# Stacking the high and low rows of a 65-row remainder into one product of a split-precision Gram stage

## The reference

```
sq = jnp.sum(xyz * xyz, axis=1)
d2 = sq[:, :, None] + sq[:, None, :] - 2.0 * jnp.einsum('bdn,bdm->bnm', xyz, xyz)
_, idx = jax.lax.top_k(-d2, k)                    # k = 8
...
shortcut = points
p = _lrelu(points)
g = _group_point(p, idx_t)                        # the 8 neighbours' columns
c = jnp.einsum('oi,bin->bon', w_center[i], p)
gn = jnp.einsum('oi,bikn->bokn', w_neighbor[i], g)
points = (c + gn.sum(axis=2)) / (K + 1.0) + shortcut
```

## Time and profile before

| | |
|---|---|
| median of three runs | 321.87 us (321.72 to 322.04) |
| the profiled execution | 321.73 us, of which span 319.9 us |
| TensorE clock granted | 1.00 throughout |
| TensorE busy | 314.8 us (98%) |
| VectorE, ScalarE, GpSimd busy | 251.7, 172.6, 94.0 us |
| Gram stage | about 4.4 to 105 us, with the start of the layers |
| layer steps | about 110.6 us to the end |

### The profile page before, as it was taken

One profiled execution on the slowest core, in us unless ns is written; L12 is line 12 of the kernel. 1 busy time (PEld: TensorE's weight loads), 2 busy tenths in 40 slices (PEclk: granted clock), 3 DMA queues, 4 the chain that ended last, 5 costly groups with the idle time before them and its releaser, 6 DMA issues.

```text
span 319.9 us, 5033 instructions
## 1 busy us (share of the span) xinstructions
PE 314.8 (98%) x1974; PEld 287.5 (90%) x1974; DVE 251.7 (79%) x333; ACT 172.6 (54%) x255; POOL 94.0 (29%) x85
## 2 busy tenths in 40 slices
PE   8999999999999899999999999999999999999996
PEld 6999999999999688898888988888888988889885
DVE  3995799899899969998777767777776767767674
ACT  4557387388377346546584455444554455544530
POOL 2011111101126304433344333443344333443330
PEclk9999999999999999999999999999999999999999
DMA  7979959988950300000300000000000000000113
GB/s 251 315 284 198 267 166 223 237 283 190 261 92 1 66 2 0 2 0 2 66 1 2 1 3 0 0 0 2 0 2 0 2 0 0 2 0 2 67 67 134
DMA packets 17313, 25.52 MB, mean 80 GB/s; under 512 B 9476, under 2 KB 10756, under 8 KB 17288
## 3 DMA queue, kind: packets, MB, share of 16 engines
q1 hardware_dynamic: 15992, 20.46, 21.3%
q0 software_dynamic: 1296, 4.72, 8.2%
HBM read 20.98 MB, written 2.10 MB: 72 GB/s over the span
## 4 chain that ended last, share of the span: by engine, by line
PE 96%; DVE 2%; DMA 1%; issue 0%; ACT 0%; DVEq 0%
PE wide L444 38%; PE wide L323 29%; PE wide L417 18%; PE wide L433 9%; DMA raw<-in_ctx_dram 1%; PE wide L385 1%; PE wide L392 1%; PE wide L373 1%; DVE gram L713 0%; DVE y_lo L757 0%; DVE r_mixed L690 0%; PE wide L396 0%; DVE half_diag L720 0%; ACT g_high L527 0%; DVE state L765 0%
## 5 line engine op out<-in xcount | busy, mean ns | idle before, releaser
L301 POOL TENSOR_TENSOR r_low<-relu,r_high 128x512 fp32r<-128x512 f32 x64 | 83.7, 1331 | 135.7 <-ACT r_high L593 135.7
L444 PE MATMUL wide<-adj,y_hi 128*128 128x512 f32 (+1 forms) x260 | 101.8, 393 | 1.2 <-DVE y_lo L757 1.2
L444 PE MATMUL wide<-adj,y_lo 128*128 128x512 f32 (+1 forms) x260 | 101.7, 393 | 0.0
L598 ACT CAST y_hi<-wide 128x1024 fp32r<-128x1024 f32 x32 | 32.6, 1018 | 89.2 <-PE wide L417 89.2
L750 DVE TENSOR_TENSOR y_rest<-wide,y_hi 128x1024 f32<-128x1024 f32 x32 | 39.1, 1223 | 30.3 <-ACT y_hi L598 30.2
L765 DVE SCALAR_TENSOR_TENSOR state<-wide,state 128x512 f32<-128x512 f32 (+1 forms) x65 | 44.1, 678 | 20.0 <-PE wide L444 19.9
L444 PEld LDWEIGHTS wide<-adj,y_hi 128*128 128x128 f32 x260 | 49.0, 188 | 10.7 <-issue 2.0
L444 PEld LDWEIGHTS wide<-adj,y_lo 128*128 128x128 f32 x260 | 48.9, 188 | 8.7
L593 ACT ACTIVATE r_high<-relu 128x512 fp32r<-128x512 f32 x64 | 40.6, 634 | 2.0
L590 ACT ACTIVATE relu<-state 128x512 f32<-128x512 f32 x64 | 40.2, 627 | 1.5 <-POOL r_low L301 1.5
L757 DVE SCALAR_TENSOR_TENSOR y_lo<-wide,y_rest 128x1024 fp32r<-128x1024 f32 x32 | 39.1, 1222 | 0.0
(11 more groups left out here) (57 smaller groups left out, 285.7 us busy)
## 6 DMA issues: line engine op xcount, KB each, us to landing
raw<-in_ctx_dram SPq DMA_DIRECT2D x23, 512.0 KB, 5.5
g_low<-in_ctx_dram POOLq DMA_DIRECT2D x9, 512.0 KB, 7.9
state<-in_x_dram SPq DMA_DIRECT2D x4, 512.0 KB, 8.9
out_dram<-state SPq DMA_DIRECT2D x3, 512.0 KB, 2.8
w_raw<-in_fside_BxSxS_dram SPq DMA_DIRECT2D x1, 1024.0 KB, 7.8
rest_raw<-in_ctx_dram SPq DMA_DIRECT2D x4, 130.0 KB
raw<-in_ctx_dram SPq DMA_DIRECT2D x2, 256.0 KB, 3.2
turned<-nbr SPq DMA_TRANSPOSE x16, 3.1
```

What stands on the lines that cost most here:

```text
L301: nc.gpsimd.tensor_tensor(r_low[:, n % 3, h, :], relu[:, h, :], r_high[:, n % 3, h, :].bitcast(fp32), ALU.subtract).then_inc(r_low_ready, 1)
L444: mm = nc.tensor.matmul(bank[to][:, cols], part[:, s % 2, q, h * P:(h + 1) * P], adj[:, b, q, cols], start=(q == 0 and part is y_hi), stop ...
L598: nc.scalar.copy(y_hi[:, s % 2, :, :], wide[main_at(s)][:, :].rearrange("p (q o) -> p q o", q=NB))\
```

## The change

For the first 64 of the 65 rows of the rest, high and low parts are put one above the other in a new tile `rest_both` (rows 0 to 63 high, 64 to 127 low). One product of 128 rows then gives hh + ll of those rows. The 65th row is left over. Its low and high part are put twice below the 65 mixed rows in a new tile `rest_left`, as rows 65 to 68, and their counterparts in `rest_mixed` are multiplied by -SHIFT and by -1, so that the mixed product of 69 rows adds -(SHIFT + 1)(hh + ll) of that row, which UNMIX turns into hh + ll.

The rows go to other partitions by DMA. GpSimd issues five DMAs per item (`rest_copies`): 64 rows of the high part, 64 rows of the low part, twice 2 rows of 512 (4 KB), and the 65 rows of the mixed part (130 KB). ScalarE multiplies rows 64 to 68 by a column of factors (`last_rows`). TensorE's `main_products(b, 6)` waits for the first two DMAs and has one group of four matmuls where there were two, and `mixed_products(b, 6)` waits for ScalarE. `rest_high` and `rest_low` become halves of one tile. VectorE sets the factors at the start (three memsets). The load of the next item's rest also waits for the last-row copies. Two pairs of calls change places at the start of the layers: `copy_adj(2)` goes ahead of `copy_low(3)` on ScalarE, and `y_low(0)` ahead of `relu_mixed(1)` on VectorE.

```
+        rest_parts = sb("rest_parts", [P, 2, N], fp32r)
+        rest_low, rest_high = rest_parts[:, 0, :], rest_parts[:, 1, :]
+        rest_both = sb("rest_both", [P, N], fp32r)
+        rest_left = sb("rest_left", [P, N], fp32r)
+        factors = sb("factors", [P, 1], fp32)
...
         # SP, load_unit, b > 0, k == 6
                         sp.wait_ge(main_summed, b * NB)
+                        sp.wait_ge(last_rows_landed, 32 * b)
...
+            def rest_copies(b):
+                if b > 0:
+                    pool.wait_ge(main_summed, b * NB)
+                pool.wait_ge(g_high_ready[PAIRS], b + 1)
+                pool.dma_start(rest_both[0:HALF, :], rest_high[0:HALF, :]).then_inc(rest_both_landed, 16)
+                pool.wait_ge(g_low_ready[PAIRS], b + 1)
+                pool.dma_start(rest_both[HALF:P, :], rest_low[0:HALF, :]).then_inc(rest_both_landed, 16)
+                if b > 0:
+                    pool.wait_ge(mixed_summed, b * NB)
+                for first in (REST, REST + 2):
+                    pool.dma_start(rest_left[first:first + 2, :], rest_parts[HALF:REST, :, :]).then_inc(last_rows_landed, 16)
+                pool.wait_ge(g_mixed_ready[PAIRS], b + 1)
+                pool.dma_start(rest_left[0:REST, :], rest_mixed[0:REST, :]).then_inc(rest_left_landed, 16)
...
+            rest_copies(0)
             for b in range(1, B):
                 for k in BY_DMA:
                     points_low(b, k)
+                rest_copies(b)
             for n in range(B * LAYERS):
                 relu_low(n)
...
             def main_products(b, k):
+                if k == PAIRS:
+                    pe.wait_ge(rest_both_landed, 32 * (b + 1))
+                    for i in ROWS:
+                        product(i, [rest_both], 0, MAIN_BANK, start=False, stop=True).then_inc(main_summed, 1)
+                    return
...
             def mixed_products(b, k):
+                if k == PAIRS:
+                    pe.wait_ge(rest_scaled, b + 1)
+                    for i in ROWS:
+                        nc.tensor.matmul(sums_of(i, MIXED_BANK), rest_left[0:LEFT, i * P:(i + 1) * P],
+                                         row_of(i, rest_mixed[0:LEFT, :]), start=False, stop=(i != ROWS[0]))\
+                            .then_inc(mixed_summed, 1)
+                    return
...
+            def last_rows(b):
+                act.wait_ge(factors_set, 3)
+                act.wait_ge(last_rows_landed, 32 * (b + 1))
+                act.wait_ge(rest_left_landed, 16 * (b + 1))
+                nc.scalar.mul(rest_mixed[HALF:LEFT, :], rest_left[HALF:LEFT, :], factors[HALF:LEFT, 0:1])\
+                    .then_inc(rest_scaled, 1)
...
             points_parts(1, 3)
+            last_rows(0)
             weights_high(2)
...
                     points_parts(b + 1, 2)
+                    last_rows(b)
                     points_parts(b + 1, 3)
...
                     relu_parts(1)
+                    last_rows(b)
                     copy_main(b)
...
                 if s == 1:
+                    copy_adj(B - 2)
                     copy_low(B - 1)
-                    copy_adj(B - 2)
...
             diagonals(B - 1)
+            y_low(0)
             relu_mixed(1)
-            y_low(0)
```

More of the change, by code:

```diff
@@ L53, in knn_blocks_kernel @@
     SHARE = (1.0 + 1.0 / SHIFT) / (K + 1)
-    assert PAIRS == 6 and 0 < REST <= P and NB == 4 and CH == 2 and K == 8
+    assert PAIRS == 6 and 0 < REST == P // 2 + 1 and NB == 4 and CH == 2 and K == 8
     UNITS = PAIRS + 1
+    HALF = P // 2
+    LEFT = REST + 4
     BY_DMA = (1, 3, 5)
@@ L93, in knn_blocks_kernel @@
             pass
-        rest_low = sb("rest_low", [P, N], fp32r)
-        rest_high = sb("rest_high", [P, N], fp32r)
+        rest_parts = sb("rest_parts", [P, 2, N], fp32r)
+        rest_low, rest_high = rest_parts[:, 0, :], rest_parts[:, 1, :]
+        rest_both = sb("rest_both", [P, N], fp32r)
+        rest_left = sb("rest_left", [P, N], fp32r)
         rest_mixed = sb("rest_mixed", [P, N], fp32r)
+        factors = sb("factors", [P, 1], fp32)
         gram = sb("gram", [P, NB, N], fp32)
@@ L180, in knn_blocks_kernel @@
         first_in = sem("first_in")
+        rest_both_landed = sem("rest_both_landed")
+        rest_left_landed = sem("rest_left_landed")
+        last_rows_landed = sem("last_rows_landed")
+        factors_set = sem("factors_set")
+        rest_scaled = sem("rest_scaled")
         unit_in = [sem(f"unit_in_{k}") for k in range(UNITS)]
@@ L345, in main_products @@
                     for i in ROWS:
[L346 to L350, removed]
-            def mixed_products(b, k):
+                        mm = product(i, low, t, MAIN_BANK, start=False)
+                mm.then_inc(main_used, 1)
+            def mixed_products(b, k):
+                if k == PAIRS:
[5 more added lines that the diff above has]
+                    return
                 mixed = tiles_of(k, g_mixed, rest_mixed)
@@ L359, in mixed_products @@
                             pe.wait_ge(gram_ready, (b - 1) * NB + FREED[n])
[L360 to L364, removed]
+                        mm = product(i, mixed, t, MIXED_BANK, start=(k == 0 and t == 0))
+                mm.then_inc(unit_used, 1)
             def turn_weights(l):
@@ L766, in update @@
                                                op0=ALU.mult, op1=ALU.add).then_inc(state_ready, 1)
+            nc.vector.memset(factors[HALF:P, :], -1.0).then_inc(factors_set, 1)
+            dve.wait_ge(factors_set, 1)
+            nc.vector.memset(factors[HALF:REST + 2, :], -SHIFT).then_inc(factors_set, 1)
+            dve.wait_ge(factors_set, 2)
+            nc.vector.memset(factors[HALF:REST, :], 1.0).then_inc(factors_set, 1)
             for k in range(UNITS):
```

## The result

The changed kernel takes 326.93 us (median of four runs, 325.86 to 328.56), the kernel before 321.87: a ratio of 1.0145, with a 95% interval of 1.0116 to 1.0174. It is slower by about 5 us. The forecast was 320.2 us, with a range up to 324.0, and is wrong in its sign as well as in its size. The profiled execution took 327.0 us, of which the span is 325.2.

A forecast was written before the change was run, and what follows sets the result against it. TensorE was taken as the bound, busy 314.8 of 319.9 us. Three items gaining 0.59 each (1.77) less 0.1 lost at the join gave -1.7 us, so 320.2 us for the median, range 319.0 to 324.0.

The forecast's parts named there:

- The size is that of the first, so I take 2.4: Mixed-row copy, issue to landing: 2.4 us, from the 1.8 us row of 128 KB plus 0.3 and 0.3.
- 4 or more: Upper end for the mixed copy's landing in the loaded first item, in us: half of 7.9.
- Four matmuls of any number of rows cost 0.59: TensorE's rest products: row count does not matter, so one group of four fewer gives 0.59 us per item.
- Issue 0.65 for the large, 0.45 for the small: GpSimd's price in us per new DMA issue; four from the low part on take 2.2, ends 1.2 and 3.5.
- The bare condition: Second and third item: the mixed part must land before 50.1; at 51.1 TensorE loses 1.0 for 0.59 gained.
- the first rival: Flat 0.87 us issues make ScalarE wait and TensorE wait for `main_copied`: sum +2.4, 324.2 us; chance 0.25.
- The prediction's own signs of being wrong: TensorE waits over 0.6 us per item for `main_copied` or rest copies, or join steps over 1 us off 110.7 less 1.77.
- First item, "no wait": Mixed part lands at 24.6, or by 26.2, before ScalarE wants it at 26.27: just covered, 0.59 us gained.
- Last item and join: Uncovered GpSimd issues delay the join: TensorE starts at 110.7 instead of 110.62, so the item's 0.59 us is given back.
- The layer steps unchanged: The layer steps after the join: forecast change 0 us.
- GpSimd's descriptors wait for VectorE: Rival: each issue waits for a 1.22 us VectorE instruction, mixed part lands 4.9 later: beyond 330 us; chance 0.03.
- the forecast's own chain: Whole kernel: three items gain 0.59 each, 1.77 in all, and the join loses 0.1, so -1.7 us.

The follow-up runs named there:

- the late-rows kernel: The changed kernel with ScalarE's `last_rows` of the second and third item put behind the main copies: 321.02 us, ratio 0.9958 to the kernel before.
- without the 32 bytes: The changed kernel with an unused 32-byte tile added, taking `adj` and the weights off the multiple of 64 bytes: 330.47 us, ratio 1.0238 to the kernel before.

## Why the prediction was wrong

The step that failed is the landing of the mixed copy in the second and third item: "The size is that of the first, so I take 2.4". Measured there: 5.0 and 5.5. The two rows that it chose between were 1.8 us for 128 KB with little beside it and 6.3 to 8.8 for 512 KB amid the loads; it went by the size, and what decides is whether a load goes out with the copy. The size was no bad guide as long as none did: 2.2 us for 65 rows with the load held back, and 2.2 for the 64 rows issued 1.6 us ahead of the load. It had the right bound of "4 or more" in hand and used it for "the loaded first item" alone.

The load could have been found beforehand. The forecast issues the mixed copy at 47.47; the timeline of the kernel before has, in a row that the prediction does not read:

```profile
47.55 0.33 SPq L241 DMA_DIRECT2D raw<-in_ctx_dram  x1
```

This load of 512 KB waits for VectorE's `g_mixed` of unit 4, which follows the rest's parts directly, and the copy is the fourth of the issues, about 0.5 us each, that the first of these parts sets off. So the two meet by the order of the kernel: in the second and third items after, with the adding DMA held back, and with `last_rows` later, the load follows the copy by 0.10 to 0.12 us each time.

Point by point:

- *Four matmuls of any number of rows cost 0.59*: right (50.82 to 51.41).
- *Issue 0.65 for the large, 0.45 for the small*: measured 0.53 and 0.51, in the sum 2.1 instead of 2.2 for the four from the low part on. The price hardly depends on the rows (2 or 65), but it is not the 0.87 that the rival took. Right in what matters.
- *The bare condition, "the mixed part must land before 50.1"*: right, and it is what makes the case readable. In the frame of before (0.62 less) it landed at 52.8, 2.9 later than forecast, of which 2.6 are the landing and the rest a later issue. The mechanism of the first rival, ScalarE's wait in place of the matmuls, then went off as it was written: two items with TensorE waiting for `main_copied`, 1.95 us each. The rival had a chance of 0.25 and the price 324.2, since it mis-sized the same landing (2.6) and put the lateness down to the issues, which took 0.5 each. The prediction's own signs of being wrong came: waits of more than 0.6 us for `main_copied`, and steps that start 10 us away from 110.7 less 1.77.
- *First item, "no wait"*: the second of the two stacked copies took 5.6 us and TensorE waited 0.88 for it; in the late-rows kernel it did not wait and the item gave its 0.58. The cover there is thin and depends on when the loads come.
- *Last item and join*: right but for the clock. `y_rest` to the end of `y_lo` took 119.21 - 113.53 = 5.7 us, forecast 5.4; the start of the steps is some 0.3 late against a forecast of 0.1.
- *The clock*: not in the prediction at all, since the earlier trace rows and the page before had 1.00 throughout. A wait of TensorE was priced at its own length throughout; the two of 1.95 us cost about 3.7 each.
- *The layer steps unchanged*: wrong by 3.4 us, in the change's favour. Nothing in the diff's arithmetic says so; its three new tiles do.
- *GpSimd's descriptors wait for VectorE*: did not happen; the 20 issues took 0.51 to 0.72 us each with VectorE busy 77% of the time. In which port mode VectorE's instructions ran no view shows, so "the trace does not agree" says more than it can: these instructions held up no issue, and the rule itself is not tested.

That the result was not worse was luck: without the 32 bytes it is 330.5 us. With the landing, the waits and the clock put in at their measured sizes the forecast's own chain gives nearly all of it: -1.7 as forecast, +3.9 of waits for the copies, +0.85 for `last_rows`, +0.88 for `rest_both`, +3.5 of clock is +7.4 of the +8.2 to +8.7 that the start of the steps shows. The rest, about 1 us, is spread over restarts after the waits and loads that came a little later; it was not resolved.

## What to carry to other kernels

A copy between tiles costs what goes out beside it: here 130 KB took 2.2 us with no load behind it and 5.0 with a 512 KB load issued 0.11 us later. So look, in the trace before, for what the other queue issues at the time at which the copy will be issued. Put the instruction that waits for the copy as late as its engine's order allows, and count what stands behind it. A wait of the bounding engine of about 2 us can cost nearly twice its length where the clock falls after it. Before a small gain is credited to a change, look whether groups that the diff doesn't touch have changed their time, and where its new tiles pushed the others.

## What the hardware showed that was not expected

- Matmuls whose moving operand begins at a multiple of 64 bytes in its partition are faster than with 32 bytes more: 1.81 instead of 1.89 us for 16 of 256 columns, 3.4 us over 32 layer steps, shown in both directions by a 32-byte tile.
- An issue on GpSimd costs 0.51 us for 2 rows, 0.53 for 64 or 65 (0.55 to 0.72 for the first of the five in each item), and 0.87 for the 128 rows of 4 KB of an adding DMA.
- A copy of 130 KB issued 0.11 us ahead of a 512 KB load on another queue took 5.0 us to land, and 2.2 with the load held back. A copy of 4 KB took 1.5 to 1.9 us in the second item, ahead of the load, and 4.3 and 4.9 in the first, amid loads.
- The granted clock fell from 1.00 to about 0.7 over the 6 us after a wait of 1.95 us on TensorE, twice in one execution, and to 0.57 for 4 us after three waits of 1.1 to 1.2 us close together at the join.
- GpSimd's subtraction for the layers, 1.33 us each, took 4.26 us for two at the join after, with VectorE's `r_mixed` at 2.31 instead of 1.22 beside it.

```profile
108.21 4.26 POOL L332 TENSOR_TENSOR r_low<-relu,r_high 128x512 fp32r<-128x512 f32 x2 [0.21 <-ACT r_high L640]
...
109.01 2.31 DVE L740 SCALAR_TENSOR_TENSOR r_mixed<-r_low,r_high 128x1024 fp32r<-128x1024 f32 x1
```
